# GpSimd copies the two slot columns of a token tile and waits for the copy ahead of its pair of scatters, and of gathers in the late attention

## The reference

```python
x = L0_attn_x
xn = _layernorm(x)
x = x + causal_softmax_attention(xn, Wq, Wk, Wv) + _L0_ffn_ref(xn, ...)
xn = _layernorm(x)
x = x + _L1_attn_ref(xn, W_qkv, W_out) + _L1_ffn_ref(xn, ...)

def _L0_ffn_ref(x, Wr, br, W1, b1, W2, b2):      # 8 experts, 2 of them per token
    routing = softmax(x @ Wr + br)
    topk_vals, topk_idx = jax.lax.top_k(routing, 2)
    topk_norm = topk_vals / jnp.sum(topk_vals, axis=-1, keepdims=True)
    gate = jnp.sum(one_hot(topk_idx, E) * topk_norm[..., None], axis=2)
    h = relu(einsum('bsd,edh->ebsh', x, W1) + b1)
    y = einsum('ebsh,ehd->ebsd', h, W2) + b2
    return einsum('ebsd,bse->bsd', y, gate)
```

## Time and profile before

| | us |
|---|---|
| median of 3 runs | 980.91 (980.83 to 981.66) |
| the profiled execution | 979.83 |
| its span, first to last instruction | 978.2 |
| PE busy | 865.8 (89%) |
| DVE busy | 674.3 (69%) |
| ACT busy | 515.4 (53%) |
| POOL busy | 181.2 (19%) |

### The profile page before, as it was taken

The page is one execution under the profiler, slowest core; times in us unless marked ns, Lnnn a source line. Parts: engine busy times, 40 slices in busy tenths (PEclk is TensorE's granted clock), DMA queues, the critical chain, the costliest instruction groups (busy, mean ns, idle before and its releaser), DMA issues. The chain is left out here.

```text
span 978.2 us, 16165 instructions
## 1 busy us (share of the span) xinstructions
PE 865.8 (89%) x5619; PEld 773.9 (79%) x5619; DVE 674.3 (69%) x1287; ACT 515.4 (53%) x907; POOL 181.2 (19%) x198
## 2 busy tenths in 40 slices
PE   3898202799799999999999999999979999999998
PEld 3687101799699999899999989999878787978877
DVE  7786000454666878878787787888477979889764
ACT  3632000433555564664756465475438867678581
POOL 1004775000000000000000000000612526153202
PEclk9999555899999999999999999999989999999999
DMA  8772446000544766666567665653300203021101
GB/s 263 265 253 76 151 156 218 1 1 2 163 131 150 230 229 214 214 220 209 190 207 244 216 211 203 221 197 103 92 23 22 65 19 98 16 76 53 43 1 44
DMA packets 93871, 134.24 MB, mean 137 GB/s; under 512 B 8608, under 2 KB 78688, under 8 KB 93824
## 3 DMA queue, kind: packets, MB, share of 16 engines
q1 hardware_dynamic: 85024, 107.80, 33.6%
q0 software_dynamic: 8800, 25.83, 7.9%
HBM read 98.22 MB, written 35.39 MB: 137 GB/s over the span
## 5 line engine op out<-in xcount | busy, mean ns | idle before, releaser
L1061 PE MATMUL ps<-w2h,hh 128*128 128x256 f32 x568 | 162.8, 287 | 0.0
L1063 PE MATMUL ps<-w2h,hl 128*128 128x256 f32 x568 | 160.7, 283 | 0.0
L1062 PE MATMUL ps<-w2l,hh 128*128 128x256 f32 x568 | 160.7, 283 | 0.0
L1201 ACT ACTIVATE h<-ps,b1T 128x512 f32<-128x512 f32 (+1 forms) x160 | 90.5, 588 | 132.7 <-PE ps L1063 132.5
L1306 DVE TENSOR_TENSOR hl<-h,hh 128x512 fp32r<-128x512 f32 x124 | 85.5, 689 | 66.1 <-ACT hh L1205 65.2
L1061 PE MATMUL ps<-xTh,w1h 128*128 128x512 f32 (+1 forms) x320 | 110.7, 346 | 2.4 <-DVE xTl L1248 2.4
L1050 POOL DMA_DIRECT2D expert_out<-y x28 | 20.5, 733 | 492.3 <-DVE y L1265 492.3
L1062 PE MATMUL ps<-xTl,w1h 128*128 128x512 f32 (+1 forms) x320 | 110.6, 346 | 0.0
L1061 PEld LDWEIGHTS ps<-w2h,hh 128*128 128x128 f32 x568 | 108.7, 191 | 2.4 <-DVE hl L1306 0.2
L1062 PEld LDWEIGHTS ps<-w2l,hh 128*128 128x128 f32 x568 | 108.8, 192 | 2.1
L1063 PE MATMUL ps<-xTh,w1l 128*128 128x512 f32 (+1 forms) x320 | 109.9, 343 | 0.0
(11 more groups left out here) (306 smaller groups left out, 2262.9 us busy)
## 6 DMA issues: line engine op xcount, KB each, us to landing
raw<-in_L_ffn_W SPq DMA_DIRECT2D x30, 1024.0 KB
raw_odd<-in_L_ffn_W SPq DMA_DIRECT2D x28, 1024.0 KB, 6.8
dispatched<-shared SPq DMA_DIRECT2D x1, 9088.0 KB, 32.1
expert_out<-y POOLq DMA_DIRECT2D x11, 512.0 KB, 3.6
rows<-dispatched SPq DMA_DIRECT2D x20, 256.0 KB, 3.4
shared<-in_L_ffn_b SPq DMA_DIRECT2D x9, 512.0 KB, 8.3
xn_rows<-raw SPq DMA_DIRECT2D x4, 1024.0 KB, 5.2
rows<-xn_rows SPq DMA_DIRECT2D x32, 128.0 KB
```

Of the source, the lines that this page charges most:

```text
L1061: pe.matmul(out, ah, bh, start=start, stop=False, skip_group_check=True)
L1062: pe.matmul(out, ah, bl, start=False, stop=False, skip_group_check=True)
L1063: return pe.matmul(out, al, bh, start=False, stop=stop, skip_group_check=True)
L1201: op = act.activation(h32[:, at, cols], ps[:, slot, cols], ACT.Relu, bias=s.b1T[:, ds(e * HC + w * tile.chunks + n, 1)])
```

## The change

On GpSimd, in part one, each pair of scatters is preceded by a copy of its two slot columns into one of four places of a new tile `places`, and the first scatter of the pair waits for that copy; the scatters take their row numbers from the copy. In part three the eight pairs of gathers for sequence 0 get the same with a new tile `picked`; the gathers of `gather_beside` stay as they were. Two semaphores are added (`placed`, `copied`) and two saved: the memset of `zero` counts in `padded`, and `den_clipped` and `den_inv` become one, `den_step`, that counts both steps.

```diff
-            pool.memset(zero[:, :], 0.0).then_inc(zero_ready, 1)
+            pool.memset(zero[:, :], 0.0).then_inc(padded, 1)
...
-            sp.wait_ge(zero_ready, 1)
+            sp.wait_ge(padded, 3)
...
             for t in range(NT):
                 pool.wait_ge(row_loaded[t % 4], 16 * (t // 4) + 16)
+                pool.tensor_copy(places[:, t % 4, :], s.slots[:, K * t:K * t + K]).then_inc(placed, 1)
+                pool.wait_ge(placed, t + 1)
                 for k in range(K):
-                    slot = s.slots[:, K * t + k:K * t + k + 1]
+                    slot = places[:, t % 4, k:k + 1]
                     pool.indirect_dma_start(out=dispatched, out_offset=bass.IndirectOffsetOnAxis(ap=slot, axis=0),
                                             in_=xrow[:, t % 4], in_offset=None).then_inc(scattered[t % 4], 16)
...
+            def gather_from_copy(i):
+
+                pool.tensor_copy(picked[:, i, :], s.slots[:, K * i:K * i + K]).then_inc(copied, 1)
+                pool.wait_ge(copied, i + 1)
+                for k in range(K):
+                    pool.indirect_dma_start(
+                        out=s.picked_rows[:, i, k, :], out_offset=None, in_=expert_out,
+                        in_offset=bass.IndirectOffsetOnAxis(ap=picked[:, i, k:k + 1], axis=0)
+                    ).then_inc(s.gathered[i], 16)
...
             pool.wait_ge(s.last_stored, 16)
-            gather(pool, s, expert_out, 0, 0)
+            gather_from_copy(0)
...
             for i in range(1, BT):
-                gather(pool, s, expert_out, 0, i)
+                gather_from_copy(i)
...
-                    V.tensor_scalar(den[:, n % 2], nd[:, :, :, P:P + HP], 1e-6, None, ALU.max).then_inc(den_clipped, 1)
-                    dve.wait_ge(den_clipped, NG * b + n + 1)
-                    V.reciprocal(den[:, n % 2], den[:, n % 2]).then_inc(den_inv, 1)
-                    dve.wait_ge(den_inv, NG * b + n + 1)
+                    V.tensor_scalar(den[:, n % 2], nd[:, :, :, P:P + HP], 1e-6, None, ALU.max).then_inc(den_step, 1)
+                    dve.wait_ge(den_step, 2 * (NG * b + n) + 1)
+                    V.reciprocal(den[:, n % 2], den[:, n % 2]).then_inc(den_step, 1)
+                    dve.wait_ge(den_step, 2 * (NG * b + n) + 2)
```

More of the change, by code:

```diff
@@ L181, in norm_route_attend @@
         cnt = sb("cnt", [P, MT])
+        places = sb("places", [P, 4, K], U32)
         xrow = s.rows[:, :, :, :].rearrange("p u s d -> p (u s) d")
@@ L188, in norm_route_attend @@
         w_loaded, small_loaded = sem("w_loaded"), sem("small_loaded")
-        const_ready, zero_ready, zero_filled = sem("const_ready"), sem("zero_ready"), sem("zero_filled")
+        const_ready, placed, zero_filled = sem("const_ready"), sem("placed"), sem("zero_filled")
         padded = sem("padded")
@@ L1382, in combine_and_layer1 @@
         same_head, head_of = sb("same_head", [P, P]), sb("head_of", [P, HP])
+        picked = sb("picked", [P, BT, K], U32)
         wout = sb("wout", [P, DC, D])
@@ L1404, in combine_and_layer1 @@
             "qT_mm", "qT_ready", "kv_mm", "kv_ready", "v_mm", "gated"))
-        nd_mm, den_clipped, den_inv, att_ready, att_turned, oT_ready = (sem(n) for n in (
-            "nd_mm", "den_clipped", "den_inv", "att_ready", "att_turned", "oT_ready"))
+        nd_mm, den_step, att_ready, att_turned, oT_ready = (sem(n) for n in (
+            "nd_mm", "den_step", "att_ready", "att_turned", "oT_ready"))
         wh_ready, wl_ready, xh_ready, xl_ready = (sem(n) for n in ("wh_ready1", "wl_ready1", "xh_ready1", "xl_ready1"))
         out_mm, out_added, final, stored = (sem(n) for n in ("out_mm", "out_added", "final", "stored"))
-        gate_added, last_final = sem("gate_added"), sem("last_final")
+        gate_added, last_final, copied = sem("gate_added"), sem("last_final"), sem("copied")
         _, kl_ready, proj_mm, proj_hi, proj_lo = s.projecting
```

## The result

The changed kernel took 971.6 us (median of 4 runs, 967.42 to 973.48) against 980.87 (4 runs, 979.96 to 981.66): ratio 0.9899, 95% interval 0.9877 to 0.9922. It is 9.3 us faster, not 76: the sign of the forecast is right, and its size is off by a factor of eight. The profiled execution took 967.42, with a span of 965.8 us; it is the fastest of the four. Of the experiments' executions one, among the ten of the first experiment, took 1774.22 us and is left out of all that follows.

What follows compares the result with a forecast made beforehand. Dense scatters on POOL starve PE, ACT and DVE: 979.83 - 71.5 (stall) - 6 (late gathers) + 1 (late scatters) + 0.5 (den_step) + 0.2 (first gather copy) = 904.0, plus 1.08 for the median: 905 us. The 80% range is 897 to 984.

Steps and rivals of the forecast that it cites:

- What bounds the kernel: About 98 to 171 us: POOL's back-to-back scatters leave PE, ACT and DVE issuing nearly nothing; the stall costs 71.5 us.
- full relief: Copies before scatter pairs in part one prevent the stall, 71.5 us back; 905 us in all, range 897 to 917, chance 0.45.
- The debt: Each scatter adds 0.14 us of unfinished service; others run freely below 1.4 us; with the change it reaches 0.9.
- S: Service that only one can have at a time, left by each scatter: 1.408 us, or 1.430 from part three's gathers.
- the sign of being wrong: The forecast is wrong if scatters are spaced wider than 2.8 us per pair and the others starve all the same.
- Delta: Time that copy and wait add on POOL before each pair of scatters: 0.22 us; below 0.205 the relief fails.
- partial relief: Part one's stall begins later, near 113 us, and still ends near 174: 958 us, about 939 to 970; chance 0.26.
- DVE's help: Sequence 1's two subtractions, the first at 123.4 us, slow scatters by 0.5 us each, taking 1.0 us off the debt.
- What comes late next: Scatters end at 173.1, rows arrive by 182.2, PE would begin part two at 182.0: cover used up, 1 us charged.
- The late gathers: Part three, copies before 8 pairs of gathers: ACT's wait of 5.96 us comes back, a gain of 6 us.
- den_step: Adds 2 register instructions to 4 divides in 2 rounds, 16 in all: 0 to 4.8 us, 0.5 taken.
- The slower rival: Part one's stall lasts as long as the scatters, ending 9.26 us after the last one: 990 us; chance 0.19.

Runs made afterwards that it cites:

- the first experiment: The changed kernel with the 8 late pairs of gathers issued without a copy, against the kernel before: 977.6 us (ratio 0.9966).
- the repeat: The changed kernel, unchanged, run again where the kernel before takes 980, against the kernel before: 972.68 us (ratio 0.9914).
- a copy before each: The changed kernel with a one-column copy and wait before every single scatter instead of each pair: 935.95 us (0.9541 against the kernel before).
- seven copies: The changed kernel with seven copies and waits before every fourth pair of scatters, none before the others: 921.16 us (0.9396), 911.85 us (1.0123) where nothing stalls.
- two copies: The changed kernel with the copy and wait done twice before each pair of scatters: 921.53 us (0.9412 against the kernel before).
- four copies: The changed kernel with the copy and wait done four times before each pair of scatters: 930.87 us (0.9497 against the kernel before).
- free group: A group of runs in which the kernel before has no hole and took 900.2 us (10 runs) or 901.0 us (7 runs).
- stalling group: A group of runs in which the kernel before has the hole and took 980.5 to 980.9 us (medians of 13, 13 and 7 runs).

## Why the prediction was right and wrong

**What bounds the kernel: right.** Three engines with work at hand wait for nothing but the scatters' density. With the scatters replaced by memsets or plain DMAs the hole is gone, in a group where the kernel before took 980.6. The price was right too: part one is 252.1 - 177.4 = 74.7 us longer than where nobody starves (72.3 to 75.5 over all the traces without a hole; 71.5 forecast), part three 285.5 - 280 = 5.5 (6 forecast). The forecast of full relief, 905, is what such a kernel takes.

**The debt with S = 1.408 us and a free limit of 1.4 us: the step that failed.** It was fitted to a stretch in which the others do almost nothing. It said that above 1.408 us per scatter nobody starves, and that the others run freely while the debt is under 1.4 us. In the changed kernel PE stood still at 98.2 us, 5.2 pairs in, with a debt by this arithmetic of 5.2 x 0.098 = 0.5 us. Of the 71.5 us that were to come back, 10.1 came (4.4 in the repeat). Measured, with the added pause worked out from the spacing:

| kernel | added pause | us per scatter | end of part one | us |
|---|---|---|---|---|
| before | none | 1.268 | 252.1 | 980.9 |
| changed | 0.18 per 2 scatters | 1.359 | 241.9 (247.7 when run again) | 971.6 |
| a copy before each | 0.20 per 1 | 1.468 | 212.9 | 936.0 |
| seven copies | 1.65 per 8 | 1.474 | 192.8 | 921.2 |
| two copies | 0.46 per 2 | 1.500 | 193.5 | 921.5 |
| four copies | 0.96 per 2 | 1.748 | 177.4 | 930.9 |

At 1.468, above S, 35 us are still lost, at 2.94 us per pair, which is the sign of being wrong that the prediction gave (wider than 2.8); the loss is zero only at 1.748. That the others' own instructions use up some of what the scatters take, so that a S read while they starve is too low for when they run, would explain it; it is argued, not shown. What is left of the debt is its sign: pauses win several times their length (59 us for 13, 75 for 30, but 4 to 10 for 6 at the low end), and a stall goes on past the last scatter. Its end, forecast at 64 x 1.408 = 90.1 us after the first scatter's start whatever the gap, came at 171.60 - 84.17 = 87.4 and, in the repeat, at 178.00 - 87.55 = 90.5. With 64 rows per scatter they ended 4.1 us earlier than with 128 half rows (162.13 against 166.22, both from a start at 85.55), and ACT came back only 2.4 us earlier (173.19 against 175.58).

**Delta: 0.22 forecast, 0.18 measured.** The pieces were each right within 0.03, and their sum fell below the 0.205 at which the prediction itself said that full relief fails. Its rival of partial relief, at delta 0.18, would give about 27 us in part one by the same arithmetic (1.4 / 0.098 = 14 pairs of 2.72 us, less the 12.3 us), so some 948, with a stall that begins at 84.2 + 39 = 123 us. 10.1 came, and the stall began at 98.2. The partial rival's range, 939 to 970, ends near the measured 971.6, but by luck: the relief came from more instructions during the stall, not from a later beginning.

**DVE's help:** it never came to act, since the stall began at 98 us, long ahead of the subtraction that was to pay off 1.0 us. The changed kernel's run in a free group shows its size:

```profile
122.43 1.22 DVE L835 TENSOR_TENSOR xl<-xnT_early,xh 128x1024 fp32r<-128x1024 f32 x1
```

```profile
122.92 1.57 POOL L317 DMA_INDIRECT dispatched<-rows,places  x1 [0.30 <-issue]
```

The subtraction comes where it was forecast (123.4), and the scatter beside it takes 1.57 us instead of 0.97, 0.6 more (0.5 forecast). Beside the second one, at 127.88, no scatter is longer than 0.99: the one at 127.68 had started before it. So 0.6 of the 1.0 us came. With half rows and no copies, in the same group, a scatter beside each of the two is longer (1.55 and 1.36 us), 1.0 in all.

**What comes late next: right, and under-priced.** In a free group the changed kernel is 3.7 us slower, with PE waiting for rows that the longer scatters delay; the forecast charged 1 us.

**The late gathers:** 6 us forecast, 2.0 to 2.5 measured in part three. The gap there was near the same (0.46 us). Whether a longer one gives more, no run in a stalling group shows.

**den_step:** with the late gathers as before, part three took 285.8 us against 285.5, and 284.9 to 285.6 in the kernels built on the one before: too little to tell from nothing. Forecast 0.5.

**The slower rival** (the stall lasts as long as the scatters) fell: the last scatter ended 5.7 us later and ACT came back 2.7 us earlier. In the repeat, counted from the first scatter, the scatters lasted some 6 us longer and ACT came back 0.4 us later. The rule behind it, from "Perfetto Trace Analysis", section "DMA Instruction — SWDGE (GPSIMD)", in the Trainium skill, that the profiled end is the end of descriptor writing, explains none of this: ACT came back 9.26 us behind the last scatter's end before, and 171.60 - 170.75 = 0.85 us (3.67 in the repeat) behind it after, with the same transfers.

"SBUF — State Buffer", section "Who interferes with whom", in the Trainium skill, names one pair of ports as the only place where engines hinder each other, and says that PE and ACT never wait on anyone there. That may hold for PE's and ACT's ports, which no run here measured. It must not be read as "GpSimd's DMAs leave PE and ACT alone": ACT's 80.62 us above are the counter-example.

**Still open.** What it is in an indirect DMA that takes the others' instructions; and why groups of runs differ by 80 us. It isn't the chip alone: on one chip the kernel before took 900.2 in one group and 980.6 in a later one.

## What to carry to other kernels

When several engines start one instruction every 0.7 to 2 us with work at hand while GpSimd sends indirect DMAs back to back, spread these out, 1.5 us per DMA here, better with one pause of 1.65 us in eight than with a sliver before each, until what waits for the last one becomes the bound. Measure such a pause where the stall is and where it isn't: the same pauses were worth 6% in one group of runs and cost 1.2% in another. A margin of 0.02 us in a term that is multiplied by 32 isn't a forecast: test the constant at another density before building on it.

## What the runs showed of the hardware that I had not expected

- 64 indirect DMAs at 1.27 us each cost the other engines 75 us of work, and the same number of plain DMAs from the same queue, at 0.83 us each, or of memsets at 1.09 us, left no hole (905.8 and 905.3 us).
- Halving the bytes or the rows of each scatter changes nothing (981.1 and 981.6 us, one run each).
- 64 rows cost GpSimd nearly what 128 do: 1.201 us per scatter against 1.265 to 1.268.
- The same program takes 900 or 980 us depending on the group of runs, and stays at the one for the 7 to 13 runs of a group.
- The stall ends without a packet in the instruction queues: none from 106 to 188 us, and 64 matmuls from 174 to 188.
- A scatter that starts while DVE subtracts with both inputs in SBUF takes 1.57 us in place of 0.97.
- A memset of 128x1024 on GpSimd takes 1.08 us (18.33 / 17); a copy behind a copy with a wait between costs 0.25 us more ((0.93 - 0.19) / 3).
